# Loading the second half of each expert's first weight from ScalarE's queue

## The chip, the cores and the metric

One core of a Trainium2 chip runs the program. The time is that of one execution on the device in microseconds, the median of three runs. TensorE is called PE here, VectorE DVE, ScalarE ACT, GpSimd POOL and SyncE SP; SP only issues DMAs and waits.

## The reference

A transformer block on 4096 tokens of width 256, modulated by six rows that come from a condition vector. An attention part (sliding window of 128, a memory that is updated by one gradient step, two gates) is followed by a mixture of experts. The last stage computes the routed experts: each token goes to its 8 best of 64 experts, an expert takes at most 160 tokens, and each computes

```python
h = jnp.einsum('ech,efh->ecf', buf, expert_w1)      # 256 -> 2 x 768
x1, x2 = jnp.split(h, 2, axis=-1)
out = jnp.einsum('ecf,ehf->ech', x1 * jax.nn.silu(x2), expert_w2)   # 768 -> 256
```

whose rows, times the gate of the token, are added to the output. All arithmetic is in float32. An expert's first weight is 256 x 1536 floats (1536 KB), its second 768 x 256 (768 KB).

## The kernel before, in words

The kernel has three stages: one that computes the attention and the memory's gradient tile by tile, one that computes the gates, the shared expert and the routing, and scatters each token's row into its slots in DRAM, and the last one, `expert_stage` (line 2000), which goes over the 64 experts. Each engine has a program of its own in this stage, a `step(n, q, i)` for expert n; the first eight and the last eight steps are written out, those between are a loop of eight steps (`experts`, line 2040). The engines meet only by semaphores, and the order of work on each engine is the order in its step.

PE (`tensor`, line 2251) does for expert n: the transposes of its rows x (`turn_x`), the second half of the first product of expert n - 1 (`up(n - 1, 1 - p, 1)`, 24 matmuls), the first half of the first product of n (`up(n, p, 0)`, 24 matmuls, which wait for the first weight, line 2311), and the second product of n - 1 (`down`, 18 matmuls, three for each of six parts: the operands are split in a high and a low part). A profile shows the two `up` as one block of 48 matmuls at line 2036. An expert has 128 rows of its own and 32 more ("rest"); the rest of four experts is multiplied together in `down_rest`, once in four steps, as 48 narrow matmuls.

ACT (`scalar`, line 2114) copies the transposed rows out of PSUM, makes the silu and gating copy of the second half of n - 1 (`silu`, `g_high`), then the silu of the first half of n, waits for the second weight, rounds it (line 2142) and makes the next gating copy. DVE multiplies the halves (line 2158), makes the low parts, and scales the results (`y_rows`, `rest_rows`). POOL (`gpsimd`, line 2206) adds the results to the output: for each expert one add of 128 rows and one of 32, and the next expert's adds wait until these have landed. At every fourth expert POOL also waits for the scaled rest of that group of four.

All loads of the stage are issued by SP (`sync`, line 2075), in one order: for expert n the rest's rows (for four experts at once), x, the token numbers, then the first weight, then the second weight. The first weight has two buffers, so its load for n waits until the four blocks of expert n - 2 are multiplied (`sp.wait_ge(S("h_mm"), (n - 1) * 4)`, line 2096). The second weight and x have eight buffers. x of n waits until the adds of expert n - 8 have landed. For the first eight experts SP also waits, ahead of everything else of n, until the scatters that fill that expert's slots have landed; POOL issues these scatters in the same stage, up to the start of its adds. The first weights of experts 0 and 1 and the second weight of expert 0 are loaded before the stage begins (`first_weights`, line 2068).

The first weight lies in DRAM in pieces of 768 floats: four to a partition, two for each half of the 256 inputs. A DMA raises its semaphore by 16 when all of it has landed.

Of the kernel before, what the change touches and what calls it, by code (L numbers as in the profile page):

```python
# [25 lines left out]
DC = D // P  # L26
# [10 lines left out]
E = 64  # L37
TOPK = 8
HELD = 5
FFN = 768  # L40
# [4 lines left out]
RING = 8  # L45
REST = CAP - P
PIECE = 768
# [1952 lines left out]
def expert_stage(nc, ctx, T, buf, held, psum, S, B):  # L2000
# [56 lines left out]
    def in_pieces(tile):  # L2057
        return tile.rearrange("p k n -> p (k n)").rearrange("p (c f) -> p c f", f=PIECE)

    def load_w1(sp, n, p):  # L2060
        sp.dma_start(in_pieces(w1[p][:]), T["e1T"][bass.ds(n, 1)].rearrange("a c p f -> p (a c) f"))\
          .then_inc(S(f"w1_in{p}"), 16)

    def load_w2(sp, n, q):
        sp.dma_start(in_pieces(w2[q]), T["e2T"][bass.ds(n, 1)].rearrange("a c p f -> p (a c) f"))\
# [2 lines left out]
    def first_weights(sp):  # L2068

        sp.wait_ge(B("lin_mm"), 4 * CHUNKS)  # L2070
        for n in range(2):
            load_w1(sp, n, n)
        load_w2(sp, 0, 0)

    def sync(sp):
        def load_rest(n, q):
            sp.dma_start(x_rest[q // QUAD][quarter(q % QUAD), :], slot_rows(T, n, P, REST))\
              .then_inc(S(f"rest_in{q}"), 16)

        def step(n, q, i):  # L2080
            first = isinstance(n, int) and n < RING
            if first:
                sp.wait_ge(B(f"level{n}"), 16 * TPC)
                if n >= HELD:
                    sp.wait_ge(B(f"held{n}"), 16 * TPC)
                load_rest(n, q)
            elif q % QUAD == 0:
                sp.wait_ge(S("y_rest"), quad_of(q, i) - 1)
                for j in range(QUAD):
                    load_rest(n + j, q + j)  # L2090
            wait_past(sp, S("added"), (n - RING + 1) * 32)
            sp.dma_start(x[q][:], slot_rows(T, n, 0, P)).then_inc(S(f"x_in{q}"), 16)
            sp.dma_start(token_rest[q][:], slot_rows(T, n, P, REST)[:, D + E - 1:ROW]).then_inc(S(f"token_in{q}"), 16)
            if not first or n >= 2:

                sp.wait_ge(S("h_mm"), (n - 1) * 4)
                load_w1(sp, n, q % 2)
            if not first or n >= 1:
                if not first:
                    wait_past(sp, S("rest_mm"), quad_of(q, i) - 1)  # L2100
                load_w2(sp, n, q)
            if isinstance(n, int) and n == 1:
                sp.wait_ge(B("base"), 2 * CHUNKS)
                out_rows = T["out"][0:TOKENS, :].rearrange("(c t p) d -> p (c t) d", p=P, t=TPC)
                sp.dma_start(out_rows[:, TOKENS // P - TPC:TOKENS // P, :], last_base(buf)).then_inc(S("base_out"), 16)

        of_all = 16 * TPC * TOPK * (CHUNKS // 2 - 1)
        sp.wait_ge(B("row_out0"), of_all)
        sp.wait_ge(B("row_out1"), of_all + 16 * TPC * HELD)
        sp.wait_ge(B("gT_low"), CHUNKS * FC)  # L2110
        experts(sp, step)
        sp.wait_ge(S("added"), E * 32)

    def scalar(act):
        def silu(n, g):
            act.wait_ge(S("h_mm"), 4 * n + 2 * g + 1)

            wait_past(act, S("gT"), 2 * n - 1 + g)
            act.activation(flat(sil[:, g * H:(g + 1) * H, :]), psum[1 + 2 * g][:, 0:H * CAP], ACT.Silu)\  # L2119
               .then_inc(S("sil"), 1)  # L2120

        def g_high(n, q, g):
            act.wait_ge(S("gT"), 2 * n + g + 1)

            wait_past(act, S("y_mm"), n - 1)
            act.copy(gTs[q % 2][0][:, g * H:(g + 1) * H, :], gT[q][:, g * H:(g + 1) * H, 0:P]).then_inc(S("g_high"), 1)  # L2126

        def step(n, q, i):
            p = q % 2
            act.wait_ge(S("xT_mm"), n + 1)  # L2130
            wait_past(act, S("h_mm"), (n - 1) * 4)
            by_block = psum[0][:, 0:2 * DC * P].rearrange("p (s k t) -> p s k t", s=2, k=DC)
            act.copy(xT[p][:, :, 0:P], by_block[:, 0])  # L2133
            act.copy(xT[p][:, :, P:CAP], by_block[:, 1, :, quarter(q % QUAD)]).then_inc(S("xT"), 1)
            if not isinstance(n, int) or n >= 1:
                silu(n - 1, 1)
                g_high(n - 1, (q - 1) % RING, 1)
            silu(n, 0)
            act.wait_ge(S(f"w2_in{q}"), (i + 1) * 16)

            wait_past(act, S("y_mm"), n - 1)
            act.copy(flat(w2s[p][0][:]), flat(w2[q])).then_inc(S("w2_high"), 1)
            g_high(n, q, 0)

        experts(act, step)
        silu(E - 1, 1)
        g_high(E - 1, RING - 1, 1)
# [103 lines left out]
    def tensor(pe):  # L2251
        def turn_x(n, q, i):
            first = isinstance(n, int) and n < RING
            p, j = q // QUAD, q % QUAD
            pe.wait_ge(S(f"x_in{q}"), (i + 1) * 16)
            wait_past(pe, S("xT"), n)
            for k in range(DC):
                ins = nc.tensor.transpose(psum[0][:, k * P:(k + 1) * P], x[q][:, k * P:(k + 1) * P], ident[:])  # L2258
            if first:
                pe.wait_ge(S(f"rest_in{q}"), 16)  # L2260
                for k in range(DC):
                    at = (DC + k) * P + j * REST
                    ins = nc.tensor.transpose(psum[0][:, at:at + REST], x_rest[p][quarter(j), k * P:(k + 1) * P],
                                              ident[quarter(j), quarter(j)])
            elif j == 0:
                for r in range(q, q + QUAD):
                    pe.wait_ge(S(f"rest_in{r}"), (i + 1) * 16)
                for k in range(DC):
                    ins = nc.tensor.transpose(psum[0][:, (DC + k) * P:(DC + k + 1) * P],  # L2269
                                              x_rest[p][:, k * P:(k + 1) * P], ident[:])  # L2270
            ins.then_inc(S("xT_mm"), 1)

        def up(n, p, g):
            for part in range(2):

                wait_past(pe, S("sil" if part == 0 else "gT"), 2 * n - 1 + g)
                for j in range(H):
                    col = ((FC if part == 0 else 0) + g * H + j) * P
                    for k in range(DC):
                        ins = mm(psum[1 + 2 * g + part][:, j * CAP:(j + 1) * CAP], w1[p][:, k, col:col + P],  # L2280
                                 xT[p][:, k, :], k == 0, k == DC - 1)
                ins.then_inc(S("h_mm"), 1)

        def down(n, p):

            pe.wait_ge(S("w2_low"), n + 1)
            wait_past(pe, S("y"), n - 1)
            for k in range(FC):
                if k % H == 0:
                    pe.wait_ge(S("g_low"), 2 * n + k // H + 1)  # L2290
                ins = mm_split(nc, psum[Y_BANK[p]][:, 0:D], cut(gTs[p], slice(None), k, slice(None)),
                               cut(w2s[p], slice(None), k, slice(None)), k == 0, k == FC - 1)
            ins.then_inc(S("y_mm"), 1)

        def down_rest(p, group, js):
            wait_past(pe, S("y_rest"), group)
            for k in range(FC):
                for j in js:
                    q = p * QUAD + j
                    ins = mm(psum[Y_REST_BANK][quarter(j), 0:D], gT[q][:, k, P:CAP], w2[q][:, k, :],  # L2300
                             k == 0, k == FC - 1)
            ins.then_inc(S("rest_mm"), 1)

        def step(n, q, i):
            p = q % 2
            static = isinstance(n, int)
            late = not static or n >= 1
            turn_x(n, q, i)
            if late:
                up(n - 1, 1 - p, 1)  # L2310
            pe.wait_ge(S(f"w1_in{p}"), (i * (RING // 2) + q // 2 + 1) * 16)
            pe.wait_ge(S("xT"), n + 1)
            up(n, p, 0)
            if late:
                if static and n == 1:
                    pe.wait_ge(B("base_raw"), 2 * CHUNKS)
                down(n - 1, 1 - p)
            if q % QUAD == 0 and (not static or n >= QUAD):
                down_rest((q // QUAD + 1) % 2, quad_of(q, i) - 1, range(QUAD))
            if static and n == E - 2:  # L2320
                down_rest(1, QUADS - 1, range(0, 2))

        experts(pe, step)
        up(E - 1, 1, 1)
        down(E - 1, 1)
        down_rest(1, QUADS, range(2, QUAD))
# [98 lines left out]
```

## Time and profile before

| | us |
|---|---|
| median of 3 runs | 1845.57 (1841.81 to 1849.28) |
| the profiled execution, its time | 1846.72 |
| its span, first to last instruction | 1844.5 |
| PE busy | 1794.9 (97%) |
| DVE busy | 1217.2 (66%) |
| ACT busy | 947.0 (51%) |
| POOL busy | 937.6 (51%) |

The profile comes from one execution. Busy times of PE are modelled, since its matmuls are pipelined. A wait is put down to what ended last before the waiting instruction started. The DMAs of SP run on hardware queue q1, the adds of POOL on software queue q0, and both on the same 16 DMA engines. The last stage starts at about 1200 us; in slices of a fortieth of the span the DMA engines are busy there 80% to 90% of the time, against 10% to 30% before.

### The profile page before, as it was taken

The numbers are of one execution on the slowest core, as the hardware profiler recorded it, in microseconds if no ns is written. First come the engines' busy times: TensorE is split into PE (matmuls) and PEld (weight loads), VectorE is DVE, ScalarE is ACT, GpSimd is POOL, SyncE is SP. The second block draws the span as 40 slices with busy tenths as digits, with TensorE's granted clock in tenths as the row PEclk, the third lists the DMA queues.
The fourth block names the chain that finished last, engine by engine and source line by source line (L and its number), as shares of the span: only waits on it lengthen the run. The fifth ranks groups of instructions, "written<-read, shape, count | busy, mean of one in ns | idle before, by whom it ended". The sixth has DMA issues, their size and how long they took to land.

```text
span 1844.5 us, 35719 instructions
## 1 busy us (share of the span) xinstructions
PE 1794.9 (97%) x12168; PEld 1579.0 (86%) x12168; DVE 1217.2 (66%) x2253; ACT 947.0 (51%) x1792; POOL 937.6 (51%) x699
## 2 busy tenths in 40 slices
PE   7899999999999999999999999999999999999995
PEld 5788888888888887787788877889999999999994
DVE  7877777777777777766777668745555555555552
ACT  5666666666666664635444344343444434444341
POOL 6566666666666664035666666654233323333234
PEclk9999999999999999999999999999999999999998
DMA  7111111111111101311111103168898888888883
GB/s 238 59 46 36 38 35 41 35 35 38 35 43 51 36 30 38 113 60 30 47 46 47 45 2 103 51 221 263 288 286 287 284 277 283 289 289 285 274 289 85
DMA packets 141022, 234.16 MB, mean 127 GB/s; under 512 B 24756, under 2 KB 88971, under 8 KB 140816
## 3 DMA queue, kind: packets, MB, share of 16 engines
q1 hardware_dynamic: 116368, 220.50, 35.0%
q0 software_dynamic: 24576, 12.69, 4.6%
q8 instruction: 40, 0.66, 0.2%
q14 instruction: 38, 0.31, 0.1%
HBM read 194.58 MB, written 78.45 MB: 148 GB/s over the span
## 4 chain that ended last, share of the span: by engine, by line
PE 54%; DMA 2%; issue 1%; DVE 1%; POOL 0%; ACT 0%; SPq 0%; POOLq 0%; DVEq 0%; ACTq 0%
PE bank L86 26%; PE bank L2036 23%; PE bank L1300 4%; DMA out_rows<-c_y_rest,c_token_rest 2%; PE bank L2258 1%; PE bank L1799 1%; DMA c_w<-in_e1T 0%; DMA slots<-last_row,last_index 0%; POOL out_rows L2210 0%; PE bank L2269 0%; POOL slots L1995 0%; DVE early L1678 0%; DVE c_y_rest L2177 0%; DVE b_h_low L1581 0%; POOLq L2344 0%
## 5 line engine op out<-in xcount | busy, mean ns | idle before, releaser
L2036 PE MATMUL bank<-c_xT,c_w 128*128 128x160 f32 x3072 | 429.6, 300 | 3.2 <-DMA c_w<-in_e1T 2.5
L2036 PEld LDWEIGHTS bank<-c_xT,c_w 128*128 128x128 f32 x3072 | 419.2, 190 | 4.3 <-DMA c_w<-in_e1T 3.2
L1995 POOL DMA_INDIRECT slots<-b_row,b_index x224 | 251.2, 1121 | 192.3 <-issue 116.4
L2210 POOL DMA_INDIRECT out_rows<-c_y,c_x x64 | 101.2, 1581 | 375.2 <-DMA out_rows<-c_y_rest,c_token_rest 275.0
L2158 DVE TENSOR_TENSOR c_gT<-bank,c_sil 128x480 f32<-128x480 f32 x128 | 84.1, 657 | 211.1 <-PE bank L2036 211.1
L2126 ACT CAST c_gTs_high<-c_gT 128x384 fp32r<-128x384 f32 x128 | 65.6, 513 | 135.3 <-DVE c_gT L2158 135.3
L2119 ACT ACTIVATE c_sil<-bank 128x480 f32<-128x480 f32 x128 | 73.0, 570 | 110.0 <-PE bank L2036 109.5
L2151 DVE TENSOR_TENSOR c_gTs_low<-c_gT,c_gTs_high 128x384 fp32r<-128x384 f32 x128 | 71.5, 559 | 75.3 <-ACT c_gTs_high L2126 75.3
L485 POOL TENSOR_TENSOR last_row<-last_row,a_e 128x256 f32<-128x256 f32 x33 | 53.4, 1618 | 126.6 <-DVE a_e L781 126.6
L86 PE MATMUL bank<-c_w2s_high,c_gTs_high 128*128 128x256 f32 x384 | 114.1, 297 | 0.9 <-DVE c_gTs_low L2151 0.9
L86 PE MATMUL bank<-c_w2s_high,c_gTs_low 128*128 128x256 f32 x384 | 107.0, 279 | 0.0
L86 PE MATMUL bank<-c_w2s_low,c_gTs_high 128*128 128x256 f32 x384 | 107.0, 279 | 0.0
L2210 POOL DMA_INDIRECT out_rows<-c_y_rest,c_token_rest x64 | 87.0, 1360 | 19.5 <-issue 19.5
L475 POOL TENSOR_TENSOR last_row<-early 128x1024 f32<-128x1024 f32 x31 | 74.2, 2395 | 37.1 <-ACT early L621 37.1
L2133 ACT COPY c_xT<-bank 128x256 f32<-128x256 f32 x64 | 23.8, 372 | 125.0 <-PE bank L2258 87.9
L637 ACT CAST pair_high<-bank 128x512 fp32r<-128x512 f32 x66 | 35.5, 589 | 99.6 <-PE bank L979 99.6
L2151 DVE TENSOR_TENSOR c_w2s_low<-c_w,c_w2s_high 128x1536 fp32r<-128x1536 f32 x48 | 84.0, 1751 | 0.0
L478 POOL TENSOR_TENSOR early<-last_row,early 128x1024 f32<-128x1024 f32 x33 | 78.9, 2392 | 7.7 <-DVE last_row L791 3.2
L440 POOL TENSOR_TENSOR a_dz_sum<-a_dz_sum,early 128x1024 f32<-128x1024 f32 x33 | 79.6, 2414 | 3.9 <-DVE a_dz_low L768 3.9
L1504 ACT ACTIVATE early<-bank,b1c 128x512 f32<-128x512 f32 x64 | 44.0, 689 | 72.9 <-PE bank L86 71.3
L482 POOL TENSOR_TENSOR a_gp<-early 128x1024 f32<-128x1024 f32 x33 | 80.0, 2424 | 2.7
L86 PE MATMUL bank<-b_hT_high,b_s1T_high 128*128 128x512 f32 x192 | 77.7, 405 | 0.0
(346 smaller groups left out, 5454.4 us busy)
## 6 DMA issues: line engine op xcount, KB each, us to landing
c_w<-in_e1T SPq DMA_DIRECT2D x64, 1536.0 KB, 6.7
c_w<-in_e2T SPq DMA_DIRECT2D x48, 768.0 KB, 9.0
early<-in_e2T SPq DMA_DIRECT2D x16, 768.0 KB, 8.6
slots<-a_fill SPq DMA_DIRECT2D x16, 642.0 KB, 4.0
c_x<-slots SPq DMA_DIRECT2D x64, 160.5 KB, 8.5
a_x_in<-in_x SPq DMA_DIRECT2D x32, 128.0 KB, 2.0
xT_tiles<-a_xT SPq DMA_DIRECT2D x32, 128.0 KB, 1.7
swaT_tiles<-a_oT SPq DMA_DIRECT2D x32, 128.0 KB
```

Of the source, the lines that this page charges most:

```text
L86: ins = nc.tensor.matmul(out, a, b, start=first and i == 0, stop=last and i == 2, skip_group_check=True)
L440: pool.tensor_tensor(dz_sum[:], dz_sum[:], dz[:], ALU.add).then_inc(S("dz_sum"), 1)
L475: pool.tensor_tensor(h[:], zb[:], sg[:], ALU.mult).then_inc(S("h"), 1)
L478: pool.tensor_tensor(om[:], h[:], om[:], ALU.mult).then_inc(S("h_om"), 1)
L482: pool.tensor_tensor(gp[:], om[:], sg[:], ALU.add).then_inc(S("gp"), 1)
L1300: return nc.tensor.matmul(out, lhsT, rhs, start=first, stop=last, skip_group_check=True)
L1995: pool.indirect_dma_start(out=T["slots"], out_offset=bass.IndirectOffsetOnAxis(ap=index[:, t, k:k + 1], axis=0), in_=row[:, t, :], in_offs ...
L2036: return nc.tensor.matmul(out, lhsT, rhs, start=first, stop=last, skip_group_check=True)
L2119: act.activation(flat(sil[:, g * H:(g + 1) * H, :]), psum[1 + 2 * g][:, 0:H * CAP], ACT.Silu)\
L2151: return dve.tensor_tensor(out, raw, high.bitcast(F32), ALU.subtract)
L2158: dve.tensor_tensor(flat(gT[q][:, g * H:(g + 1) * H, :]), psum[2 + 2 * g][:, 0:H * CAP], flat(sil[:, g * H:(g + 1) * H, :]), ALU.mult).the ...
L2210: pool.indirect_dma_start(out=T["out"], out_offset=bass.IndirectOffsetOnAxis(ap=token, axis=0), in_=rows, in_offset=None, bounds_check=las ...
```

## The change

The load of a first weight is split into two DMAs of 768 KB, one for each half of the 256 inputs. SP still issues the first half, at the same place. ACT issues the second half of expert n + 1 in step n, behind the gating copy of the second half of n - 1 and ahead of the silu of n, with a wait on the same condition (expert n - 1 is multiplied, which frees the buffer). For experts 0 and 1 SP issues both halves. Both halves raise the same semaphore, so PE waits for 32 in place of 16.

```diff
-    def load_w1(sp, n, p):
-        sp.dma_start(in_pieces(w1[p][:]), T["e1T"][bass.ds(n, 1)].rearrange("a c p f -> p (a c) f"))\
-          .then_inc(S(f"w1_in{p}"), 16)
+    def load_w1(eng, n, p, half):
+        parts = DC * 2 * FFN // PIECE // 2
+        part = slice(half * parts, (half + 1) * parts)
+        eng.dma_start(in_pieces(w1[p][:])[:, part, :],
+                      T["e1T"][bass.ds(n, 1)].rearrange("a c p f -> p (a c) f")[:, part, :])\
+           .then_inc(S(f"w1_in{p}"), 16)
...
         for n in range(2):
-            load_w1(sp, n, n)
+            for half in range(2):
+                load_w1(sp, n, n, half)
         load_w2(sp, 0, 0)
...
                 sp.wait_ge(S("h_mm"), (n - 1) * 4)
-                load_w1(sp, n, q % 2)
+                load_w1(sp, n, q % 2, 0)
...
             if not isinstance(n, int) or n >= 1:
                 silu(n - 1, 1)
                 g_high(n - 1, (q - 1) % RING, 1)
+            if not isinstance(n, int) or 1 <= n < E - 1:
+                act.wait_ge(S("h_mm"), n * 4)
+                load_w1(act, n + 1, 1 - p, 1)
             silu(n, 0)
...
-            pe.wait_ge(S(f"w1_in{p}"), (i * (RING // 2) + q // 2 + 1) * 16)
+            pe.wait_ge(S(f"w1_in{p}"), (i * (RING // 2) + q // 2 + 1) * 32)
```

## Rows read from the trace of the kernel before

**Rows 1.** The table of stretches: busy us of each engine (instructions), granted clock, DMA share, GB/s.

```profile
1500.00:1580.00 80.00, 80.00 (x671) 77.21 (x670) 41.02 (x58) 33.32 (x59) 24.33 (x17) 1.00 0.88 283
...
1787.00:1844.00 57.00, 37.39 (x292) 34.06 (x290) 18.64 (x29) 13.04 (x23) 24.57 (x16) 0.88 0.46 112
```

**Rows 2.** List of waits, 1200 to 1840: us in total, times, longest.

```profile
PEld bank L2036 <- DMA c_w<-in_e1T: 3.2, 3, 2.1
...
PE bank L2036 <- DMA c_w<-in_e1T: 2.5, 2, 1.8
```

**Rows 3.** Timeline of the first experts: start, us, engine, line, operation [idle before, releaser].

```profile
1209.11 0.51 ACT L2126 CAST c_gTs_high<-c_gT 128x384 fp32r<-128x384 f32 x1 [1.82 <-DVE c_gT L2158]
...
1211.24 0.42 SPq L2061 DMA_DIRECT2D c_w<-in_e1T  x1
...
1218.33 3.53 PE L2036 MATMUL bank<-c_xT,c_w 128*128 128x160 f32 x24 [0.72 <-DMA c_w<-in_e1T]
...
1218.41 0.51 ACT L2126 CAST c_gTs_high<-c_gT 128x384 fp32r<-128x384 f32 x1 [1.82 <-DVE c_gT L2158]
...
1222.62 0.42 SPq L2061 DMA_DIRECT2D c_w<-in_e1T  x1
...
1230.06 3.53 PE L2036 MATMUL bank<-c_xT,c_w 128*128 128x160 f32 x24 [1.82 <-DMA c_w<-in_e1T]
```

**Rows 4.** Timeline of one expert's round in the middle, all engines.

```profile
1492.13 0.38 SPq L2061 DMA_DIRECT2D c_w<-in_e1T  x1
...
1492.69 0.38 SPq L2065 DMA_DIRECT2D c_w<-in_e2T  x1
...
1492.69 0.51 ACT L2126 CAST c_gTs_high<-c_gT 128x384 fp32r<-128x384 f32 x1 [1.75 <-DVE c_gT L2158]
...
1493.71 0.57 ACT L2119 ACTIVATE c_sil<-bank 128x480 f32<-128x480 f32 x1 [0.51 <-PE bank L2036]
...
1497.40 6.68 PE L2036 MATMUL bank<-c_xT,c_w 128*128 128x160 f32 x48
...
1500.99 0.39 SPq L2061 DMA_DIRECT2D c_w<-in_e1T  x1
...
1515.09 2.80 PE L2036 MATMUL bank<-c_w,c_gT 128*32 128x256 f32 x48
```

**Rows 5.** DMA issues, 1420 to 1500: count, KB each, median us to landing.

```profile
c_w<-in_e1T SPq DMA_DIRECT2D x8, 1536.0 KB, 6.7
...
c_w<-in_e2T SPq DMA_DIRECT2D x6, 768.0 KB, 9.0
...
out_rows<-c_y,c_x POOLq DMA_INDIRECT x8, 7.5
```

**Rows 6.** DMA queues, the view's 1527 to 1528: packets, MB, share of 16 engines.

```profile
q1 hardware_dynamic: 92, 0.26, 69.2%
...
q0 software_dynamic: 64, 0.07, 40.4%
```

**Rows 7.** Timeline of POOL, the middle and the tail.

```profile
1522.00 1.54 POOL L2210 DMA_INDIRECT out_rows<-c_y,c_x  x1 [7.89 <-issue]
...
1540.36 1.54 POOL L2210 DMA_INDIRECT out_rows<-c_y,c_x  x1 [5.99 <-DMA out_rows<-c_y_rest,c_token_rest]
...
1542.21 1.33 POOL L2210 DMA_INDIRECT out_rows<-c_y_rest,c_token_rest  x1 [0.30 <-issue]
...
1560.45 1.54 POOL L2210 DMA_INDIRECT out_rows<-c_y,c_x  x1 [7.98 <-issue]
...
1808.53 1.54 POOL L2210 DMA_INDIRECT out_rows<-c_y,c_x  x1 [6.40 <-DMA out_rows<-c_y_rest,c_token_rest]
...
1831.96 1.54 POOL L2210 DMA_INDIRECT out_rows<-c_y,c_x  x1 [2.21 <-DMA out_rows<-c_y_rest,c_token_rest]
```

**Rows 8.** DMA issues, 1808 to 1845, after the last load.

```profile
out_rows<-c_y,c_x POOLq DMA_INDIRECT x6, 3.8
```

**Rows 9.** Timeline of DVE, the last rows scaled.

```profile
1825.35 0.99 DVE L2177 SCALAR_TENSOR_TENSOR c_y_rest<-bank,c_x_rest,mod 32x256 f32<-32x256 f32 x2 [2.24 <-PE bank L2036]
```

## The prediction

> **What bounds the kernel now.** I read the views from the end backwards. The chain of waits ends in POOL's adds and is PE's before them, so the question is what bounds the last stage, the one the change touches. The table of stretches answers it [rows 1]: from 1500 to 1580 us PE is busy for all 80 of 80 us at a granted clock of 1.00, while DMA is at 0.88 and ACT at 33 of 80. From 1787 on it is busy for 37 of 57 us and what is left is POOL's chain of adds. So the stage has three parts: a start with holes, a middle that is PE alone, and a tail of POOL. The list of waits of the whole stage says how much of PE's time a weight load costs today [rows 2]: 2.5 us in two waits on the matmul side, and 3.2 us in three on the weight-load side (the same holes seen from the other queue). The timeline shows where they lie, in the first experts [rows 3]: 0.72 us before 1218.33 and 1.82 us before 1230.06. In the middle there are none. That is nearly all that an earlier first weight can give back.
>
> Why it is on time in the middle is read from one expert's round [rows 4]. SP issues the 1536 KB load at 1492.13, right behind the last matmul that read the buffer. Its user is the second half of PE's block of 48 matmuls that begins at 1497.40 and takes 6.68 us, so at 1497.40 + 3.34 = 1500.74, or 8.6 us after the issue; SP's next issue of such a load, at 1500.99, is the same point one expert later. The load lands after 6.7 us, the second weight (issued 0.56 us behind it) after 9.0 us, so 9.6 us after the first one's issue [rows 5]. The slack of the first weight is 8.6 - 6.7 = 1.9 us. In every fourth expert PE also has a block of 48 narrow matmuls (2.80 us), and the slack is 2.8 us larger.
>
> **The change part by part.** *SP's load becomes half as large* (768 KB), for 62 experts (2 to 63). It keeps its place and its waits; the issue of 0.38 us stays, since it is one instruction either way. The second weight, x and the two token loads behind it find a shorter queue in front of them. Gain in the middle: 0, because PE waits for none of them; ScalarE's one wait for a second weight is not on PE's path.
>
> *ACT gets a wait, the address arithmetic and one DMA issue.* The wait (all four blocks of the expert in front are multiplied) is met beforehand, at cost 0: the gating copy just ahead of it on ACT needs the product that DVE makes from that same last block. The issue: SP's own issues of this kind take 0.38 us and stand 0.56 us apart, register instructions included. It falls between the gating copy, which ends at 1492.69 + 0.51 = 1493.20, and the silu that starts at 1493.71 [rows 4]; ACT waits for PE in that gap of 0.51 us. So the silu moves by at most 0.56 - 0.51 = 0.05 us. What is queued behind it on ACT is that silu, the rounding of the second weight and the next gating copy; PE reads their results about an expert later, and ACT is idle for more than half of the time [rows 1]. I take 0, with 0.1 us an expert (6 us in all) as the other end if the issue takes twice as long on ACT.
>
> *The second half starts later than it did.* Issued at about 1493.2, it is 1.1 us behind SP's issue. No row of this trace shows two such queues side by side, so its landing is bounded. Below: if ACT's part were sent as early as before, 6.7 us after SP's issue, when the whole weight lands today. Above: if it gets its turn only behind all that SP has queued, the second weight included, it ends when that ends today, at 9.6 us, since the bytes are the same. Between them: with turns one to one from its own issue on, 768 KB of it and 768 KB of SP's, again 1536 KB, take 6.7 us, so it lands at 1.1 + 6.7 = 7.8 us. The nearest row is the one in which two queues do move at once, the loads and POOL's adds [rows 6]: in that microsecond 92 packets of the one and 64 of the other, so turns are taken and the smaller one is not kept waiting to the end. I take 7.8 us. That is 0.8 us inside the 8.6, so PE does not wait: cost 0 in the middle, with 9.6 - 8.6 = 1.0 us an expert as the other end. What is late next, if it goes, is PE itself, directly.
>
> *PE's wait* counts 32 in place of 16 for each weight: one instruction as before, cost 0.
>
> *The first experts.* There SP stands in front of the first-weight load of an expert waiting for the scatter of its rows, and the load goes out late: at 1211.24 and 1222.62. ACT has no such wait. It would issue its half behind the copies at 1209.11 and 1218.41 (each 0.51 us), so at 1209.6 and 1218.9: 1.6 and 3.7 us ahead of SP [rows 3]. Half of the bytes are then under way or landed when SP comes. Against 1222.62 this shortens what is left by about half of the 6.7 us less its fixed part, more than the 1.82 us that PE waits. Gain 0.72 + 1.82 = 2.5 us; from 0 (if the SP half alone is as slow) to 3.2 [rows 2]. PE is the bound from there to 1787, so this reaches the end.
>
> *The tail.* POOL's last eight experts are a serial chain, an add and its landing before the next. Beside loads a step is 6.40 + 1.54 + 0.30 + 1.33 = 9.6 us (that before 1808.53), without loads 2.21 + 1.54 + 0.30 + 1.33 = 5.4 us (that before 1831.96) [rows 7]. Only the first two steps of the tail run beside loads. The bytes beside them are the same; I take 0, from -8 us (both as if undisturbed, 2 x 4.2) to +4 us (each 2 us slower with a second queue).
>
> **Sum.** The profiled execution took 1846.72 us, 2.2 us more than its span and 1.2 us above the median of the runs. 1846.72 - 2.5 + 0 + 0 = **1844.2 us**, 0.1% below its own time and within the 0.4% that the runs of before lie apart. I call a change of less than 0.5% (9 us) no change: a measurement of this kernel can't tell it from none.
>
> **The rivals.** *The second half lands late (slower).* POOL's add of 128 rows lands 3.8 us after its issue when no load is under way and 7.5 us beside them [rows 5, 8]: a newcomer to the engines pays 3.7 us while SP's queue is full. If ACT's half is such a newcomer, it needs only 0.8 us of that to miss the 8.6 us; from there each further tenth is PE idle time in three of four experts, some 46 of the 62. At the upper end it is 46 x 1.0 = 46 us, so 1890; in the middle of what is possible, 0.6 us, 28 us and 1872. For it: the 3.7 us, and a slack that the change cuts from 1.9 to 0.8 us by my own sum. Against it: turns are seen to be taken [rows 6], and the add's extra time may belong to POOL's way of issuing. Chance 0.37, a small part of it under 9 us.
>
> *POOL becomes the bound (slower).* In the middle a round of four experts takes PE 1560.45 - 1522.00 = 38.45 us, and four of POOL's steps of 5.99 + 1.54 + 0.30 + 1.33 = 9.2 us take 36.6 [rows 7]; the rest is POOL waiting for the group. It has 1.8 us a round, 0.46 us a step. If turns against two queues cost the add more than that, every step of the 56 in the middle pays: 1 us more gives 56 x 0.54 = 30 us, so 1874. For it: the adds already pay 3.7 us for one queue. Against it: the same bytes stand in front of them, in two queues for half of the time. Chance 0.06.
>
> *The adds get earlier turns (faster).* Whole weights of 1536 KB no longer stand in one piece in front of an add. In the middle this is worth nothing; in the tail it is the -8 us above, which the last pair of POOL's steps cuts to about 5, since it waits for rows that DVE makes at 1825.35 [rows 9] and starts now at 1831.96. 1844.2 - 5 = 1839. The Trainium skill has a rule that leads here (DMA: Bandwidth & Descriptors, section Queues, rings and completion order): each DMA engine goes round the queues that have work and drains a whole packet, typically 9 to 17 descriptors, before it switches. By that rule the second half would also go ahead of the second weight and PE would never wait. The row of 92 packets beside 64 [rows 6] fits turns, but can't tell whole-packet turns from single ones. Chance 0.06, half of it past 0.5%.
>
> *The start keeps its holes*, because SP's half is late by itself there: 1846.7. Chance 0.07.
>
> **How the numbers follow.** Forecast 0.44, late half 0.37, POOL 0.06, earlier adds 0.06, holes kept 0.07. Slower by over 0.5%: 0.35 + 0.06 = 0.41. Faster by over 0.5%: 0.04 (half of the earlier adds, and a hundredth for start and tail together). Within: 0.55. The forecast's own range is 1839 to 1852 (tail -5 to +4, ACT's issue up to +6). For 8 in 10 it must reach into the late half: up to 1880, which leaves out the upper quarter of that case and a little at the bottom: 1839 to 1880.
>
> **What would show it.** Right: the two holes at 1218 and 1230 gone from the list of waits; no wait of PE for in_e1T between 1260 and 1787; ACT's issue about 1.1 us behind SP's, its load landing within 7.5 us of its own issue. Wrong: PE idle on in_e1T in three of four experts, and ACT's load landing later than the second weight (rival one); a POOL step above 9.6 us and PE waiting for x (rival two); the step before 1808.53 down from 9.6 us (rival three). The sum is wrong by itself if a round of four experts in the middle is not 38.4 us.

## The result: 2.6% slower, and the profile after

The changed kernel takes 1893.49 us (median of 4 runs, 1891.35 to 1896.65) against 1847.42 us for the kernel before in the same series: a ratio of 1.026, with a 95% interval of 1.0242 to 1.0278. The forecast was 1844.2 us. The time lies at the upper end of the first rival ("the second half lands late", 1890), above the range. The profiled run took 1891.35 us, its span is 1889.0 us (before: 1846.72 and 1844.5), so the trace has 44.5 us to account for.

The table of stretches of the changed kernel, with the columns of [rows 1]; the last row is the tail, 45 us later than it was:

```profile
1500.00:1580.00 80.00, 74.62 (x623) 70.86 (x622) 38.16 (x53) 31.17 (x54) 23.27 (x16) 1.00 0.84 273
1210.00:1260.00 50.00, 49.04 (x394) 45.95 (x393) 24.14 (x34) 19.56 (x34) 33.33 (x30) 1.00 0.78 260
...
1832.00:1889.00 57.00, 35.56 (x277) 31.99 (x275) 17.15 (x25) 12.14 (x21) 24.05 (x16) 0.87 0.44 109
```

PE, busy for 80 of 80 us in the middle before, now idles for 5.4 of 80 at the same granted clock of 1.00, and DMA's share falls with it from 0.88 to 0.84: no other engine took over as the bound. The tail is as it was (35.6 us of PE in 57, before 37.4). The list of waits from 1200 on, with the columns of [rows 2], names the releaser:

```profile
PE bank L2036 <- DMA c_w<-in_e1T: 37.8, 28, 2.5
```

28 waits for a first weight in place of 2, 37.8 us in place of 2.5. The list of DMA issues from 1420 to 1500, with the columns of [rows 5], says which half it is:

```profile
c_w<-in_e1T SPq DMA_DIRECT2D x7, 768.0 KB, 4.4
c_w<-in_e1T ACTq DMA_DIRECT2D x7, 768.0 KB, 8.9
c_w<-in_e2T SPq DMA_DIRECT2D x5, 768.0 KB, 7.2
...
out_rows<-c_y,c_x POOLq DMA_INDIRECT x7, 7.9
```

SP's half lands 4.4 us after its issue, and the second weight, which stood behind the whole first one, now after 7.2 us instead of 9.0. ACT's half, of the same size, takes 8.9. The timeline of the round that answers to [rows 4]:

```profile
1486.83 0.38 SPq L2063 DMA_DIRECT2D c_w<-in_e1T  x1
1487.39 0.38 SPq L2068 DMA_DIRECT2D c_w<-in_e2T  x1
1487.39 0.51 ACT L2130 CAST c_gTs_high<-c_gT 128x384 fp32r<-128x384 f32 x1 [1.75 <-DVE c_gT L2165]
1487.62 0.38 ACTq L2063 DMA_DIRECT2D c_w<-in_e1T  x1
1487.95 3.52 PE L2036 MATMUL bank<-c_xT,c_w 128*128 128x160 f32 x24 [1.29 <-DMA c_w<-in_e1T]
...
1496.46 6.69 PE L2036 MATMUL bank<-c_xT,c_w 128*128 128x160 f32 x48
...
1500.05 0.38 SPq L2063 DMA_DIRECT2D c_w<-in_e1T  x1
...
1500.84 0.38 ACTq L2063 DMA_DIRECT2D c_w<-in_e1T  x1
```

ACT's issue leaves 0.79 us behind SP's and only 0.23 us behind the second weight's. It does not even wait for the gating copy to end: the copy starts at 1487.39 and takes 0.51 us, the issue goes out at 1487.62. Over the 15 rounds from 1420 to 1580 that half lands 8.7 to 9.3 us after its own issue, so 9.5 to 10.1 us after SP's issue; PE wanted it after 8.6. The chain of waits (start, us, what) shows what now sets the pace, this load and PE's work behind it in turn:

```profile
1478.53 9.21 DMA c_w<-in_e1T
...
1487.95 3.52 PE bank L2036 x24
...
1500.84 9.06 DMA c_w<-in_e1T
...
1510.11 3.52 PE bank L2036 x24
```

From 1480 to 1570 this chain is half DMA (50.7%); before it was PE alone. Why ACT's half takes so long is read from the DMA queues, microsecond by microsecond (packets, MB, share of 16 engines; q1 is SP's queue, q10 ACT's, q0 POOL's). Four stretches of the changed kernel, 1503 to 1504, 1504 to 1505, 1505 to 1506, and the 0.26 us from 1494.43:

```profile
q1 hardware_dynamic: 148, 0.43, 105.8%
...
q1 hardware_dynamic: 126, 0.37, 94.5%
q10 hardware_dynamic: 8, 0.02, 7.8%
...
q1 hardware_dynamic: 66, 0.20, 51.0%
q10 hardware_dynamic: 58, 0.18, 43.9%
q0 software_dynamic: 13, 0.01, 8.2%
...
q10 hardware_dynamic: 16, 0.05, 46.5%
q0 software_dynamic: 16, 0.02, 38.8%
q1 hardware_dynamic: 16, 0.02, 27.3%
```

ACT's load was issued at 1500.84, and its first packet moves at 1504.66, 3.8 us later (3.7 to 4.1 us in the 15 rounds). From 1501 to 1505 SP's queue sends 30 + 105 + 148 + 126 = 409 packets, 16 of them small ones of under 512 bytes. The other 393 are 24 to 25 for each of the 16 engines: the 16 of its half (768 KB in packets of 3 KB, 256 in all) and then 8 or 9 of the second weight's 16. Only from there on are turns taken, and then strictly: in 0.26 us each queue moves 16 packets, as many as there are engines, and where one packet can be followed by the one that starts as it ends, the queues alternate packet by packet. So ACT's half first waits for some 24 packets per engine and then gets a half or a third of the turns. That is the theory to test (**order of turns**). Two rivals stand beside it: **slow queue** (a load issued by ACT takes about 8.9 us whatever is beside it) and **split cost** (two half loads, or a second queue as such, cost more than one whole load).

### The profile page after: what moved, and what is told of

The parts are those of the page before. It is cut to its first block, busy times and chain, and to the rows that moved or that the text cites. A ratio compares the mean times of both kernels' runs of the same rounds, so it can differ in the third digit from the quotient of the medians.

```text
span 1889.0 us, 35929 instructions
## 1 busy us (share of the span) xinstructions
PE 1803.2 (95%) x12168; PEld 1580.6 (84%) x12168; DVE 1217.9 (64%) x2253; ACT 947.3 (50%) x1792; POOL 939.4 (50%) x699
## 4 chain that ended last, share of the span: by engine, by line
PE 41%; DMA 15%; DVE 2%; issue 2%; POOL 0%; ACT 0%; POOLq 0%; ACTq 0%; SPq 0%; DVEq 0%
PE bank L86 23%; PE bank L2036 14%; DMA c_w<-in_e1T 13%; PE bank L1300 4%; DMA out_rows<-c_y_rest,c_token_rest 2%; DVE c_gT L2165 1%; PE bank L1799 1%; PE bank L2265 1%; DMA c_x<-slots 0%; DMA slots<-last_row,last_index 0%; POOL out_rows L2217 0%; POOL slots L1995 0%; DVE c_y_rest L2184 0%; ACTq L2063 0%; DVE early L1678 0%
## 5 line engine op out<-in xcount | busy, mean ns | idle before, releaser
L2036 PE MATMUL bank<-c_xT,c_w 128*128 128x160 f32 x3072 | 436.8, 300 | 38.5 <-DMA c_w<-in_e1T 37.8
```

Source lines behind the costliest of these rows:

```text
L2036: return nc.tensor.matmul(out, lhsT, rhs, start=first, stop=last, skip_group_check=True)
```

## The experiments

All eight are timed beside the kernel before, whose medians in the two series are 1846.27 us (22 runs; first four experiments) and 1847.17 us (27 runs; the others).

**1. Both halves from SP.** ACT's block goes, SP issues the second half right behind the first:

```
                 load_w1(sp, n, q % 2, 0)
+                load_w1(sp, n, q % 2, 1)
...
-            if not isinstance(n, int) or 1 <= n < E - 1:
-                act.wait_ge(S("h_mm"), n * 4)
-                load_w1(act, n + 1, 1 - p, 1)
```

> Both halves of the first weight from SP, one behind the other, then the second weight; ACT issues nothing. Theory 1 (order of turns: a half from ACT gets its turn only behind what SP has already queued, the second weight included): nothing is late here, both halves have landed about 6.8 us after the first one's issue, PE has no wait in the middle, 1847 us +- 5, with the two holes of the first experts back. Theory 2 (ACT's queue or its way of issuing is slow by itself): the same 1847. Theory 3 (two DMAs of 768 KB cost more than one of 1536 KB): the PE waits of the changed kernel stay, above 1870.

Measured: 1845.85 us, ratio 0.9996 (0.9986 to 1.0006). PE is busy for all of the 160 us from 1420 to 1580. The split by itself costs nothing, so the first form of the split-cost theory falls.

**2. The second weight from ACT, the whole first weight from SP** (the other way of sharing the same bytes). The edit is shown against the kernel before:

```
-            if not first or n >= 1:
-                if not first:
-                    wait_past(sp, S("rest_mm"), quad_of(q, i) - 1)
+            if isinstance(n, int) and n == 1:
                 load_w2(sp, n, q)
...
+            if not isinstance(n, int) or 1 <= n < E - 1:
+                act.wait_ge(S("h_mm"), n * 4)
+                if not isinstance(n, int) or n + 1 >= RING:
+                    act.wait_ge(S("rest_mm"), quad_of(q + 1, i) - 1)
+                load_w2(act, n + 1, (q + 1) % RING)
```

> The first weight whole from SP; at the place where the change issues the second half, ACT issues the second weight of the next expert (768 KB too). So the same second queue with the same bytes, but the late one is a load with slack. Theory 1: the first weight keeps its turn and lands within 7.8 us of its issue, the second weight lands last, some 9 us after its own issue, inside its slack: 1845 us +- 6. Theory 2: also no PE wait, unless the second weight from ACT comes after 11 us. If a second queue beside SP's, or an issue on ACT, costs by itself: above 1870.

Measured: 1856.55 us, ratio 1.0057 (1.004 to 1.0074). DMA issues, 1420 to 1580:

```profile
c_w<-in_e1T SPq DMA_DIRECT2D x17, 1536.0 KB, 7.7
c_w<-in_e2T ACTq DMA_DIRECT2D x13, 768.0 KB, 8.9
```

ACT's load is again the slow one, and here that harms nobody directly: PE's waits for a first weight come to 4.9 us in seven. But the first weight, which now shares its last turns, takes 7.7 us in place of 6.7, still inside the 8.6. ACT's first packet moves 3.8 to 4.1 us after its issue here too, when 23 to 25 of the first weight's 32 packets per engine have gone: it doesn't wait for all that was issued before it. The time is some 5 us above the range that was expected. In the trace, by ACT's copies of x, PE comes to the first expert 1.8 us behind the kernel before, is 5.0 behind at the 17th and 7.0 at the last, and POOL's last add is 8.7 behind; POOL waits 297.5 us for its adds' landings, before 275.0. So most of the loss within the stage is PE's. How much of the 10 us the second queue carries was not separated.

**3. The changed kernel with the second weight held back** until PE has done one block (12 matmuls) of the next expert, so that it is not yet in SP's queue when ACT issues:

```
             if not first or n >= 1:
...
+                if not first or n >= 2:
+                    sp.wait_ge(S("h_mm"), 4 * n + 1 - 4)
```

> The changed kernel, but SP holds the second weight back until PE has done one more block of 12 matmuls (1.6 us later), so that ACT's half is issued in front of it. Theory 1: only the first half stands in front of ACT's half; it lands 6 to 7.5 us after its own issue in place of 8.9, inside the 8.6 us of SP's issue; PE's waits in the middle go: 1845 us +- 8; the second weight lands later instead. Theory 2: ACT's half still lands 8.9 us after its issue, PE waits as before: 1890.

Measured: 1855.1 us, ratio 1.0039 (1.0024 to 1.0055): 37 of the 46 us are gone, and the time is 2 us above the range expected. DMA issues, 1420 to 1580:

```profile
c_w<-in_e1T SPq DMA_DIRECT2D x17, 768.0 KB, 4.4
c_w<-in_e1T ACTq DMA_DIRECT2D x17, 768.0 KB, 6.3
```

The queues from 1487 to 1488:

```profile
q10 hardware_dynamic: 117, 0.36, 96.9%
q1 hardware_dynamic: 17, 0.02, 5.2%
```

ACT issues at the same point of the round, 0.79 us behind SP's half. Its first packet moves at 1486.61, 2.6 us after its issue, when 209 of SP's 256 have gone (12 to 15 per engine in the rounds from 1420 to 1580, in place of 21 to 25), and from 1487 on its packets have the engines nearly to themselves, although SP's second weight was issued at 1484.87: now that one is the newcomer. ACT's half lands 6.3 us after its issue in place of 9.0, so the slow queue falls. The 9 us that stay are single misses: nine waits of PE for a first weight, 7.6 us in all, in which ACT's half took 7.9 to 9.8 us. In the one issued at 1540.01 its last packets trickle in at 6 to 8 a us from 1546 to 1549, beside 74 to 85 and more of SP's: this fits one or a few of the 16 engines that had reached the second weight first, which no view shows. What would decide that for an engine is open.

**4. A quarter of the first weight from ACT**, 384 KB, the other three quarters from SP:

```
-        parts = DC * 2 * FFN // PIECE // 2
-        part = slice(half * parts, (half + 1) * parts)
+        parts = DC * 2 * FFN // PIECE
+        part = slice(0, parts - 1) if half == 0 else slice(parts - 1, parts)
```

> The changed kernel with ACT's share cut from two of four pieces to one (384 KB), SP's share three. Theory 1: the share still waits for the same queue, but then needs half as many turns, one to one with the second weight: lands 7.3 to 8.3 us after its issue; PE's waits mostly go, from 45 us to 0 to 20: 1847 to 1867. Theory 2 with a fixed delay of ACT's queue: lands at nearly 8.9 us, 1885 and more.

Measured: 1849.32 us, ratio 1.0018 (1.0008 to 1.0027). DMA issues, 1420 to 1580:

```profile
c_w<-in_e1T SPq DMA_DIRECT2D x17, 1152.0 KB, 5.6
...
c_w<-in_e1T ACTq DMA_DIRECT2D x17, 384.0 KB, 7.1
```

Half as many bytes from ACT, at the same point, land 0.79 + 7.1 = 7.9 us after SP's issue, inside the 8.6. The newcomer's wait is paid (3.7 to 4.0 us), but the stretch of shared turns behind it is short. The 3 us that stay are small but clear of the interval; the trace has four waits of PE for a first weight, 2.0 us in all.

**5. ACT's issue ahead of the gating copy**, so that it goes out with SP's and not 0.79 us later. Only the order of two items on ACT changes (the gating copy now follows the issue):

```
                 silu(n - 1, 1)
-                g_high(n - 1, (q - 1) % RING, 1)
             if not isinstance(n, int) or 1 <= n < E - 1:
                 act.wait_ge(S("h_mm"), n * 4)
                 load_w1(act, n + 1, 1 - p, 1)
+            if not isinstance(n, int) or n >= 1:
+                g_high(n - 1, (q - 1) % RING, 1)
```

> The changed kernel with one thing moved: ACT issues the second half ahead of the gating copy in place of behind it, so at the same moment as SP issues the first half and some 0.6 us ahead of SP's second weight. Theory 1 (a half from ACT waits behind what SP has queued when it comes, then takes turns one to one): only the first half can stand in front, it lands 6.5 to 7.5 us after its issue, PE's 45 us of waits go: 1843 to 1852 us, the start's 2 us gained. Theory 2 (ACT's queue needs its 8.9 us whatever stands in front): lands 8.9 us after SP's first half, PE still waits every second expert: 1860 to 1875.

Measured: 1847.88 us, ratio 1.0002 (0.9993 to 1.0011): the whole loss is gone. The timeline of one round of this kernel:

```profile
1484.00 0.38 SPq L2063 DMA_DIRECT2D c_w<-in_e1T  x1
1484.01 0.47 ACTq L2063 DMA_DIRECT2D c_w<-in_e1T  x1
1484.56 0.38 SPq L2068 DMA_DIRECT2D c_w<-in_e2T  x1
```

Its DMA issues, 1420 to 1580:

```profile
c_w<-in_e1T SPq DMA_DIRECT2D x17, 768.0 KB, 5.8
c_w<-in_e1T ACTq DMA_DIRECT2D x17, 768.0 KB, 6.9
```

And its queues from 1487 to 1488:

```profile
q1 hardware_dynamic: 68, 0.21, 52.6%
q10 hardware_dynamic: 65, 0.20, 49.2%
```

Same queues, same sizes, same bytes; only the issue is 0.8 us earlier. ACT's half is in its turns from 1486.33 on, 2.3 us after its issue, and shares them with SP's half instead of following it. It lands after 6.9 us, about when the whole weight landed before (6.7). PE is busy for 160 of 160 us. A second queue as such costs nothing either: the split-cost theory is out.

In two of these 17 rounds ACT's issue is 0.1 us ahead of SP's. One of them in the timeline, and below it the landings of the two halves from the list of DMA issues:

```profile
1510.70 0.44 ACTq L2063 DMA_DIRECT2D c_w<-in_e1T  x1
1510.80 0.37 SPq L2063 DMA_DIRECT2D c_w<-in_e1T  x1
...
c_w<-in_e1T ACTq DMA_DIRECT2D x1, 768.0 KB, 6.0
c_w<-in_e1T SPq DMA_DIRECT2D x1, 768.0 KB, 6.4
```

Here the places are exchanged: ACT's first packet moves 1.1 us after its issue and SP's 2.1 us after its own, where in the other rounds SP's takes 1.0 us and ACT's 2.1 to 2.5. Whichever is issued second, be it by a hundredth or a tenth of a us, gets in second; no difference between the two queues themselves shows.

**6. ACT's issue at the end of its step**, some 4 to 6 us behind SP's:

```
-            if not isinstance(n, int) or 1 <= n < E - 1:
-                act.wait_ge(S("h_mm"), n * 4)
-                load_w1(act, n + 1, 1 - p, 1)
             silu(n, 0)
...
+            if not isinstance(n, int) or 1 <= n < E - 1:
+                act.wait_ge(S("h_mm"), n * 4)
+                load_w1(act, n + 1, 1 - p, 1)
```

> The changed kernel with ACT's issue moved to the end of its step, about 3 us later. Theory 1: all that SP has is queued or served by then, the half has less in front of it: lands 6 to 7.5 us after its own issue (8.9 in the changed kernel), which is 10 to 11.5 us after SP's first half; PE's wait is about 2 to 3 us in every second expert: 1900 to 1925 us. Theory 2: 8.9 us after its own issue, 13 us after SP's: above 1950.

Measured: 1904.59 us, ratio 1.0309 (1.029 to 1.0328). DMA issues, 1420 to 1580:

```profile
c_w<-in_e1T ACTq DMA_DIRECT2D x16, 768.0 KB, 5.5
c_w<-in_e1T SPq DMA_DIRECT2D x15, 768.0 KB, 4.6
```

Issued 3 to 5 us later than in the changed kernel, the same load lands in 5.5 us instead of 9.0, because most of what SP had queued is through by then (29 to 32 of 32 packets per engine ahead of ACT's first). That too speaks against the slow queue. In total it is later still, and PE waits more (44.0 us in 38). A load that came 3 to 5 us later cost only 11 us more in all, since most of the newcomer's wait and of the sharing went.

**7. ACT's half only for experts 2 to 7**, both halves from SP from then on: what the change gives at the start, without its cost.

```
-            if not isinstance(n, int) or 1 <= n < E - 1:
+            if isinstance(n, int) and 1 <= n < RING - 1:
                 act.wait_ge(S("h_mm"), n * 4)
                 load_w1(act, n + 1, 1 - p, 1)
...
                 load_w1(sp, n, q % 2, 0)
+                if not first:
+                    load_w1(sp, n, q % 2, 1)
```

> ACT issues the second half for the first experts alone (2 to 7), where SP is held up by the scatters; from expert 8 on SP issues both halves. Theory 1: the gain of the start without the price of the middle: PE waits neither at the start nor in the middle, 1844.5 us, 0.1% below before. If the gain of the start is lost again further on (POOL's chain): the same as before, 1846.

Measured: 1846.47 us, ratio 0.9999 (0.9989 to 1.0009). The stretch of the start and that of the middle:

```profile
1500.00:1580.00 80.00, 80.00 (x671) 77.20 (x670) 41.02 (x58) 34.58 (x60) 25.77 (x18) 1.00 0.87 284
1210.00:1260.00 50.00, 49.34 (x401) 46.71 (x400) 24.45 (x35) 20.08 (x35) 33.50 (x30) 1.00 0.78 261
```

PE has no wait for a first weight at all, works 49.34 of the 50 us from 1210 (before 47.34), and is 1.6 to 1.8 us ahead of the kernel before from the fifth expert to the last, by ACT's copies of x. Of that, 1.5 us reach POOL's last add in the trace, and the runs can't tell it from nothing. This is the one version that might have beaten both kernels; it is equal to the one before.

**8. The hold of experiment 3 on the kernel before**, without a split:

```
                 load_w1(sp, n, q % 2)
             if not first or n >= 1:
...
+                if not first or n >= 2:
+                    sp.wait_ge(S("h_mm"), 4 * n + 1 - 4)
```

> The kernel before with SP holding the second weight back by one block of 12 matmuls, ACT issuing nothing: what the hold alone does in the run that held it beside ACT's half. Theory 1: nothing, 1846 us +- 4, since the second weight has slack and the first is alone in front; the 8 us of that run then belong to ACT's half. If the hold itself costs, 1852 to 1856.

Measured: 1847.19 us, ratio 0.9997 (0.9988 to 1.0007). The hold neither costs nor gains, so what experiment 3 regained came from the place in the turns.

## Why the prediction was wrong

**The step that failed** is "The second half starts later than it did", and in it the value of 7.8 us. It let ACT's packets take turns one to one from ACT's own issue on. The turns are real, and one to one; what was left out is the time before the first one. ACT's first packet moved 3.7 to 4.1 us after its issue, when 21 to 25 packets per engine of SP's had gone, where SP's own first packet moves 1.0 us after its issue. By then SP's half was through, so ACT shared its turns with the second weight, x and the adds, and ended after all of the first weight and after the second (7.2 us after an issue 0.56 us behind SP's, so at 7.8). It arrived 9.5 to 10.1 us after SP's issue in place of 7.8, at or above the bound given as 9.6. The row chosen for it [rows 6] was taken in the middle of two queues' work and can't show how the later one got in. The row that pointed to it was the add's 3.8 us alone against 7.5 us beside loads [rows 5, 8], used only for the rival; that this is the same price isn't shown.

**ACT's issue** was put 1.1 us behind SP's and came at 0.79, since an issue doesn't wait for the end of the copy ahead of it. At 0.01 us it is free, at 0.79 it costs 46 us (experiment 5 against the changed kernel); so the result hangs on a term that the prediction called hidden. Hidden for ACT it was: the issue took 0.38 us there.

**The rival's sum** gave the right total by luck, with the wrong count. It had 46 experts losing 1.0 us; PE waits 28 times. In the changed kernel the copies of x on ACT (start, us, engine, line, operation), one per expert, stand like this:

```profile
1413.42 0.37 ACT L2137 COPY c_xT<-bank 128x256 f32<-128x256 f32 x1 [4.01 <-PE bank L2265]
...
1422.29 0.37 ACT L2137 COPY c_xT<-bank 128x256 f32<-128x256 f32 x1 [1.14 <-PE bank L2265]
...
1432.82 0.37 ACT L2137 COPY c_xT<-bank 128x256 f32<-128x256 f32 x1 [1.15 <-PE bank L2265]
...
1441.98 0.37 ACT L2137 COPY c_xT<-bank 128x256 f32<-128x256 f32 x1 [1.43 <-PE bank L2276]
...
1455.01 0.37 ACT L2137 COPY c_xT<-bank 128x256 f32<-128x256 f32 x1 [3.92 <-PE bank L2265]
```

Steps of 8.9, 10.5, 9.2 and 13.0 us, where the kernel before has 8.8, 8.9, 9.1 and 11.6: every second expert stalls. PE's timeline shows one stall and the unbroken block of the next expert:

```profile
1422.09 3.42 PE L2036 MATMUL bank<-c_xT,c_w 128*128 128x160 f32 x24
...
1426.91 3.52 PE L2036 MATMUL bank<-c_xT,c_w 128*128 128x160 f32 x24 [1.39 <-DMA c_w<-in_e1T]
...
1432.62 6.68 PE L2036 MATMUL bank<-c_xT,c_w 128*128 128x160 f32 x48
```

The broken block takes 3.42 + 3.52 us beside the wait, 0.26 us more than the unbroken one. The other experts are spared because the next load is triggered ahead of the stall (SP at 1486.83, PE resumes at 1487.95): a late expert gives the following load its lost time as slack. The 28 waits are 37.8 us, 1.35 us on average, and 28 times 0.26 us are another 7: 45 us. The trace is 44.5 us longer than that of the kernel before, which had 2.5 us of such waits.

**What held.** The middle had been bound by PE with 1.9 us of slack for the first weight, and the mechanism of the loss is the one that the first rival described. The start gained most of what was forecast: the holes before 1218 and 1230 [rows 3] are gone, and PE's 49.04 us from 1210 to 1260 are 1.7 above before, against 2.5 forecast. From 1278 on, PE's first wait for a late half, that is lost again. Alone, in experiment 7, PE does 2.0 us more work in the same stretch, and the time does not show it. POOL didn't become the bound: its add of 128 rows went from 7.5 to 7.9 us, and its last add is 44 us late, as PE is. The tail kept its length, and "earlier adds" brought nothing. The rule of the Trainium skill that stood beside that rival (DMA: Bandwidth & Descriptors, section Queues, rings and completion order: a whole packet of typically 9 to 17 descriptors before a switch) was taken to send the second half ahead of the second weight. It went behind the first 8 or 9 of 16, and once both queues were moving the rows show turns of a single packet of the profile, 16, 16 and 16 in 0.26 us, so the measurement differs from the rule, and it decides.

**Open.** What makes the later queue wait for its first turn is not known. From its issue to its first packet, and in packets per engine that SP's queue sent until then, it took 2.1 to 2.5 us and 3 to 5 packets 0.01 us behind SP's half (experiment 5), 2.5 to 2.8 us and 12 to 15 behind the half alone (experiment 3), and 3.7 to 4.1 us and 21 to 25 where SP's queue had been given 32 or more (the changed kernel, experiments 2 and 4). So it is no fixed time, and not always all that was issued before. Whether the engines have read something ahead or the loads are made ready one after the other, no run separates. The single misses of experiment 3 and the 10 us of experiment 2 are read from traces and not tested.

## What to carry to other kernels

A load moved to another engine's queue keeps its bytes and can lose its place. If it is issued later than what stands on the old queue, count on it to start late: here 21 to 25 packets per engine of a full old queue went first, and only then was the rate shared. Compare the landing with the user's deadline, counted from the issue that used to be in time; here 0.8 us of issue time decided over 46 us. If a load is split over two queues, issue the parts at the same moment and ahead of anything less urgent, or leave them on one queue.

## What the runs showed that was not expected

- A DMA issue on ACT goes out 0.23 us after the start of the 0.51 us copy in front of it, so while that copy still runs.
- The same 768 KB from ACT's queue land after 5.5, 6.3, 6.9 or 9.0 us, depending on when they are issued and on what SP has queued by then (experiments 6, 3 and 5, and the changed kernel).
- Two queues that are both moving took single turns here: one packet per engine from each, whether it has 3072 bytes (ACT's weight), 1284 (x) or 1024 (the adds). A queue with small packets so gets a smaller share of the bytes.
- A wait of PE costs a little more than itself: the block of 48 matmuls that it breaks took 3.42 + 3.52 us in place of 6.68.
- An issue that comes 0.01 to 0.1 us behind the other queue's gets its first turn 1 us or more later (experiment 5).
